# Query, key and value products of a two-block transformer: one step of the layernorm beside them is placed earlier

## The chip, the cores and the metric

The kernel runs on one core of one Trainium2 chip. TensorE, VectorE, ScalarE, GpSimd and SyncE each work through an instruction list of their own and meet through semaphores. In the profile they are PE (with PEld for its weight loads), DVE, ACT, POOL and SP. SP computes nothing: it issues nearly all DMAs. The metric is the device time of one execution in microseconds (us), lower is better; 2537.11 us is the median of three runs of the kernel before.

## The reference, cut to what matters

Eight batches of 512 rows of 512 float32 values go through a cross-attention block (L0) and then through a second block with self-attention, cross-attention and an MLP. The change is in the part between L0 and self-attention:

```python
def _ln(x):                                      # B, N, H = 8, 512, 512
    mu = jnp.mean(x, axis=-1, keepdims=True)
    var = jnp.var(x, axis=-1, keepdims=True)
    return (x - mu) * jax.lax.rsqrt(var + 1e-6)
x = _L0_xcond_ref(x, ...)                        # x1 in the kernel, kept in DRAM
x_norm = _ln(x) * (1 + scale_a[:, None]) + shift_a[:, None]
qkv = x_norm @ W_qkv + b_qkv                     # 512 x 1536 weights
q, k, v = jnp.split(qkv, 3, axis=-1)
```

## The kernel before, in words

The program is six stages: prepare, l0, qkv, attention, cross, mlp. Each stage has a `run` that says in which order its steps come, and every engine walks the same `run` with its own version of each step. So the order on all engines follows from where `run` places a step. Steps that need several places are generators, and `next(...)` emits their next piece. The last steps of a stage are woven with the first of the following one: `following` is the attention stage inside `Qkv.run`.

Float32 products are made of three matmuls of rounded parts (hi by hi, hi by lo, lo by hi), for each of four chunks of 128, so a product of 128 by 512 is 12 matmuls. For each batch `Qkv.run` has 12 products: m = 0 to 3 for the queries, 4 to 7 for the keys, then t = 0 to 3 for the values. They take turns in three PSUM banks. A q or k product is drained by ACT (line 1596, hi part, into `out_parts`) and then by DVE (line 1537, lo part), and SP stores both to DRAM (line 1518, 512 KB). ACT has two `out_parts` buffers in batch 0 and three later, so the drain of a product waits until the store of the product two or three before it has landed. DVE drains a value product (line 1549) and SP stores it (line 1523).

Beside the products of batch b, the layernorm of batch b+1 is made in `Norm`, 14 pieces handed out with `next(turning)`:

- piece 1: SP loads the batch's rows, 1 MB, into the one buffer `norm_x` (line 302), once PE has turned the batch before it out of that buffer and the rows of x1 are stored
- pieces 2 to 5: DVE takes statistics of four tiles (BN_STATS, line 312); the first waits for the load
- piece 6: DVE aggregates them (line 316), and POOL makes the reciprocal deviation (lines 337, 339)
- pieces 7 to 10: DVE normalises the four tiles in place (line 321)
- pieces 11 to 14: PE turns `norm_x` by transposes (line 354), ACT scales, shifts and rounds (lines 377, 379), DVE makes the lo part (line 329). These follow product m = 7 and the first three value products.

Which product a piece follows is in `STEPS_AT`, a table from m to a number of pieces. `weave(turning)` empties what is left at a batch's end. Self-attention begins to fetch its stacks of queries and keys (lines 1745 and 1748, six DMAs of 256 KB each, with a memset of DVE, line 1815) at the end of batches 3 and 4 and after m = 4 of batch 4: `next(following)`. Batch 0 also has the last rows of L0 beside it: PE projects the last four tiles between m = 5 and m = 6, and DVE adds them to the residual (line 1265).

Of the kernel before, what the change touches and what calls it, by code (L numbers as in the profile page):

```python
# [12 lines left out]
B, N, D = 8, 512, 512  # L13
# [92 lines left out]
def braid(*generators):  # L106

    left = [g for g in generators if g is not None]
    while left:
        for g in list(left):  # L110
            if next(g, StopIteration) is StopIteration:
                left.remove(g)
        if left:
            yield


def weave(*generators):
    for _ in braid(*generators):
        pass


def after(steps, generator):
    for _ in range(steps):
        yield
    yield from generator


def some(steps, generator):
    for _ in range(steps):
        next(generator, None)  # L130
        yield
# [293 lines left out]
class Prepare:  # L425
# [90 lines left out]
    def run(self, s, following):  # L516
        def splits(l, first, n):
            for i in range(first, first + n):
                s.split(self.piece_at[l] + i)
                yield  # L520

        def modulations(*sources):
            for i in sources:
                yield from s.modulation(i)

        s.begin()
        s.statistics()
        yield from braid(s.turn(0), after(1 + TT, s.parts(0)), after(2, splits(1, 0, G)), after(2, modulations(0)))
        yield from braid(s.keys(0), splits(1, G, G), s.turn(1), after(1, modulations(1)))
        yield from braid(s.values(0), modulations(2, 3), after(1, s.modulate()), some(10, following))  # L530
        yield from braid(s.parts(1), some(13, following), after(4, splits(0, 0, 2 * G)))
        yield from s.keys(1)
        yield from braid(some(1, following), s.values(1))
# [908 lines left out]
class Qkv:  # L1442


    STEPS_AT = {0: 1, 2: 2, 3: 2, 4: 1, 5: 2, 6: 2, 7: 1}

    def __init__(self, k, w, x_in, x_ready, mods_ready):
        self.k, self.w = k, w
# [24 lines left out]
    def run(self, s, following):  # L1473
        s.begin()

        def splits():
            for m in range(G):
                s.split(self.w_at + m)
                yield

        yield from braid(s.turn(0), after(Norm.HEAD, splits()))
        for b in range(B):
            turning = s.turn(b + 1) if b + 1 < B else iter(())
            for m in range(2 * G):
                if b == 0:
                    s.split(self.w_at + G + m)
                s.product(b, m)
                for _ in range(self.STEPS_AT.get(m, 0)):
                    next(turning, None)
                if b >= B - 3:  # L1490
                    weave(some(2 if b == B - 1 else 1, following))
                elif b == B - 4 and m == G:
                    next(following)
                yield
            for t in range(NT):
                s.value(b, t)
                next(turning, None)
                if b >= B - 3:
                    weave(some(2 if b == B - 1 else 1, following))
                yield  # L1500
            weave(turning)
            if B - 6 < b < B - 3:
                next(following)

# [910 lines left out]
```

## Time and profile before

| | |
|---|---|
| median of 3 runs | 2537.11 us (2529.11 to 2539.09) |
| the profiled execution's own time | 2532.49 us |
| its span (first to last instruction) | 2530.7 us |
| mean granted TensorE clock | 0.983 |
| the qkv stage in the trace | about 499 to 809 us |
| PE idle between 500 and 812 us, named waits | 8.7 us |

The busy share of an engine says how full it is. What bounds a stretch is read from who waits last there: a wait of PE counts when PE is otherwise full. Durations in the timeline are of single instructions; PE starts a 512-column matmul about every 0.23 us though each lasts about 0.39 us, since they are pipelined. In the chain, "issue" is time in which an engine waited for nothing that the trace shows.

### The profile page before, as it was taken

Reading aid. Unit: us, or ns where it says so; the run is one execution under the profiler, and the core shown is the slowest. Engines: PE = TensorE matmul, PEld = TensorE weight load, DVE = VectorE, ACT = ScalarE, POOL = GpSimd, SP = SyncE. Lnnn points to the kernel's source line nnn. Section 1 sums busy time; section 2 is a strip of 40 time slices with the busy share of each in tenths; the row PEclk is TensorE's granted clock in tenths of the full one; section 3 lists DMA queues with packets and bytes.
Section 4 is the critical chain, followed back from the end, with each engine's and each line's share of the span. In section 5 each row is a group of like instructions: output and inputs, shape, how many; then the busy total and the mean of one; then the engine's idle time right before and its main releaser. Section 6 shows DMA issues by size and latency. Waiting matters only on the chain.

```text
span 2530.7 us, 32358 instructions
## 1 busy us (share of the span) xinstructions
PE 2389.8 (94%) x12056; PEld 1675.6 (66%) x12056; DVE 1393.1 (55%) x2463; ACT 1025.3 (41%) x1831; POOL 580.2 (23%) x324
## 2 busy tenths in 40 slices
PE   6879999899999899999998899999999999999999
PEld 5656666578776344444444566666688888888887
DVE  4566666744565877777777566666642222232221
ACT  3454454423323555555554343444442332233232
POOL 2101111200000466666665311121111001101100
PEclk9899999999999899999999999999999999999999
DMA  6687787564664455656553497777431101110110
GB/s 211 192 214 221 213 222 217 165 209 176 208 206 149 106 133 129 157 134 157 131 139 89 125 237 184 204 212 202 155 88 59 59 1 59 59 58 1 59 42 17
DMA packets 261323, 354.19 MB, mean 140 GB/s; under 512 B 61027, under 2 KB 109243, under 8 KB 261166
## 3 DMA queue, kind: packets, MB, share of 16 engines
q1 hardware_dynamic: 259998, 348.27, 48.9%
q0 software_dynamic: 1168, 3.85, 0.4%
q8 instruction: 96, 1.57, 0.3%
q14 instruction: 61, 0.50, 0.1%
HBM read 233.78 MB, written 116.69 MB: 138 GB/s over the span
## 4 chain that ended last, share of the span: by engine, by line
PE 78%; DVE 7%; DMA 6%; ACT 3%; issue 3%; SPq 2%; POOL 0%; ACTq 0%; DVEq 0%; POOLq 0%
PE banks L396 40%; PE banks L2213 14%; PE banks L1913 6%; PE banks L1935 4%; PE banks L1892 4%; PE banks L1953 2%; DMA norm_x<-x 2%; PE banks L354 2%; PE banks L1322 2%; PE banks L1336 2%; PE banks L1343 2%; DVE negated_max L1827 1%; DVE negated_max L1221 1%; DVE norm_stats L312 1%; DMA norm_x<-in_x 1%
## 5 line engine op out<-in xcount | busy, mean ns | idle before, releaser
L1997 ACT ACTIVATE self_exponentials<-banks 128x512 f32<-128x512 f32 x512 | 286.3, 595 | 280.0 <-PE banks L1953 136.2
L1827 DVE TENSOR_REDUCE negated_max<-banks 128x1 f32<-128x512 f32 x512 | 330.7, 677 | 95.9 <-PE banks L1892 94.4
L2213 PE MATMUL banks<-mlp_w_down_hi,out_parts 128*128 128x512 f32 x1024 | 333.8, 389 | 0.1
L1793 POOL TENSOR_TENSOR self_exponentials<-self_exponentials,self_exponentials 128x2048 f32<-128x2048 f32 x63 | 289.7, 4599 | 187.9 <-ACT self_exponentials L1997 187.9
L337 POOL TENSOR_SCALAR norm_rstd<-norm_mean_var 128x4 f32<-128x4 f32 x32 | 8.0, 250 | 1341.6 <-DVE norm_mean_var L316 1341.6
L2170 DVE TENSOR_TENSOR out_parts<-wide,out_parts 128x512 fp32r<-128x512 f32 x128 | 92.0, 719 | 371.7 <-ACT out_parts L2242 371.7
L2232 ACT ACTIVATE wide<-banks,bias_columns 128x512 f32<-128x512 f32 x128 | 88.3, 690 | 426.0 <-PE banks L396 426.0
L1913 PE MATMUL banks<-self_query_stack,self_key_stack 98*128 98x512 f32 x512 | 232.9, 458 | 9.7 <-ACT self_exponentials L1997 6.8
L1913 PEld LDWEIGHTS banks<-self_query_stack,self_key_stack 98*128 98x128 f32 x512 | 97.2, 191 | 190.6 <-ACT self_exponentials L1997 155.8
L2213 PEld LDWEIGHTS banks<-mlp_w_down_hi,out_parts 128*128 128x128 f32 x1024 | 192.2, 188 | 40.5 <-DVE cross_last_x_rows L1265 0.5
L1892 PE MATMUL banks<-self_key_stack,self_query_stack 96*128 96x512 f32 x512 | 208.2, 410 | 9.0 <-DVE negated_max L1827 6.7
L2213 PE MATMUL banks<-mlp_w_down_lo,out_parts 128*128 128x512 f32 x512 | 199.2, 389 | 0.0
L1221 DVE TENSOR_REDUCE negated_max<-banks 128x4 f32<-128x308 f32 x256 | 121.1, 473 | 66.8 <-PE banks L396 65.9
L1935 PE MATMUL banks<-self_exponentials,self_values 128*32 128x512 f32 x1024 | 137.0, 607 | 0.5 <-ACT self_exponentials L1997 0.5
L312 DVE BATCH_NORM_STATS2 norm_stats<-norm_x 128x6 f32<-128x512 f32 x128 | 84.9, 674 | 75.6 <-DMA norm_x<-x 68.5
L377 ACT ACTIVATE wide<-banks,modulation_columns 128x512 f32<-128x512 f32 x96 | 74.6, 777 | 114.6 <-PE banks L354 109.1
L1892 PEld LDWEIGHTS banks<-self_key_stack,self_query_stack 96*128 96x128 f32 x512 | 98.8, 193 | 27.5 <-DVE negated_max L1827 10.5
L1404 ACT ACTIVATE cross_exponentials<-banks 77x512 f32<-77x512 f32 x128 | 75.6, 593 | 99.6 <-PE banks L1322 99.5
L1207 DVE SCALAR_TENSOR_TENSOR out_parts<-banks,bias_columns,out_parts 128x512 fp32r<-128x512 f32 x64 | 47.9, 748 | 118.1 <-ACT out_parts L1380 117.6
L1596 ACT ACTIVATE out_parts<-banks,bias_columns 128x512 fp32r<-128x512 f32 x64 | 44.1, 690 | 162.8 <-PE banks L396 136.0
L329 DVE TENSOR_TENSOR x_lo<-wide,x_hi 128x512 fp32r<-128x512 f32 x80 | 61.0, 763 | 88.1 <-ACT x_hi L379 88.0
L1404 ACT ACTIVATE L_exponentials<-banks 77x512 f32<-77x512 f32 x128 | 75.5, 592 | 83.9 <-PE banks L1322 83.9
(208 smaller groups left out, 5339.5 us busy)
## 6 DMA issues: line engine op xcount, KB each, us to landing
L_query_stack<-q_parts_L SPq DMA_DIRECT2D x96, 256.0 KB, 4.9
norm_x<-x SPq DMA_DIRECT2D x24, 1024.0 KB, 7.9
self_query_stack<-q_parts_self SPq DMA_DIRECT2D x96, 256.0 KB, 4.1
self_key_stack<-k_parts_self SPq DMA_DIRECT2D x96, 256.0 KB, 6.4
cross_query_stack<-q_parts_cross SPq DMA_DIRECT2D x96, 256.0 KB, 4.8
x_rows<-x SPq DMA_DIRECT2D x23, 1024.0 KB, 6.1
x<-x_rows SPq DMA_DIRECT2D x22, 1024.0 KB, 5.0
q_parts_L<-out_parts SPq DMA_DIRECT2D x32, 512.0 KB, 4.9
```

The source lines that it names most:

```text
L312: e.bn_stats(stats[:, t, :], xn[:, t, :]).then_inc(self.stats.sem, 1)
L396: mm = e.matmul(out_ap, l, r, start=i == 0, stop=i == len(terms) - 1)
L1221: e.tensor_reduce(k.nm[n % 2][:, t:GH * NT:NT], k.bank[:, bk, 0:GH * S].rearrange("p (h k) -> p h k", k=S), AX_X, ALU.max, negate=True).th ...
L1404: e.activation(self.p[:, i % self.HEADS_KEPT, :], k.bank[0:S, self.scores.of["score", i], :], ACT.Exp, scale=SCALE).then_inc(self.exp.sem, 1)
L1793: e.tensor_tensor(self.p[kt - 1][:], self.p[kt - 1][:], self.p[kt][:], ALU.add).then_inc(self.paired.sem, 1)
L1827: e.tensor_reduce(k.nm[n % 2][:, h * NT + t:h * NT + t + 1], k.bank[:, self.max_banks.of["max", i], :], AX_X, ALU.max, negate=True).then_i ...
L1892: e.matmul(k.bank[:, bk, :], self.q[n % 4][0:ST, h, t * P:(t + 1) * P], self.keys[n % 4][0:ST, h, :], start=True, stop=True).then_inc(self ...
L1913: e.matmul(k.bank[:, bk, :], self.keys[n % 4][0:ST_MAX, h, kt * P:(kt + 1) * P], self.q[n % 4][0:ST_MAX, h, :], start=True, stop=True).the ...
L1935: mm = e.matmul(k.bank[h * HD:(h + 1) * HD, bk, :], self.v[n % 3][:, kt, h * HD:(h + 1) * HD], self.p[kt][:, h, :], start=kt == 0, stop=kt ...
L1997: e.activation(self.p[kt][:, h, :], k.bank[:, self.scores.of["score", i], :], ACT.Exp, scale=SCALE).then_inc(self.exp.sem, 1)
L2170: e.tensor_tensor(h[:, 1, :], k.wides[k.wide_turns.of["up", i]][:], raw(h[:, 0, :]), ALU.subtract).then_inc(self.lo.sem, 1)
L2213: mm = e.matmul(bank, l, w, start=j == 0 and q == 0, stop=j == JC - 1 and q == 2)
```

## The change

`STEPS_AT` is changed, and the first piece of a batch's norm (the load) is taken at the end of the batch before instead of after product m = 0. For batch 1 it is taken before the loop.

```diff
-    STEPS_AT = {0: 1, 2: 2, 3: 2, 4: 1, 5: 2, 6: 2, 7: 1}
+    STEPS_AT = {1: 2, 2: 2, 3: 1, 4: 2, 5: 2, 7: 1}
...
+        def loading(b):
+            turning = s.turn(b) if b < B else iter(())
+            next(turning, None)
+            return turning
+
         yield from braid(s.turn(0), after(Norm.HEAD, splits()))
+        turning = loading(1)
         for b in range(B):
-            turning = s.turn(b + 1) if b + 1 < B else iter(())
             for m in range(2 * G):
...
             weave(turning)
+            turning = loading(b + 2)
             if B - 6 < b < B - 3:
                 next(following)
```

The lists of PE, ACT and POOL are the same, instruction for instruction; those of SP and DVE have the same instructions in another order. Lines after 1480 have numbers that are 6 higher in the changed kernel (1518 becomes 1524, 1537 becomes 1543).

SP at the start of batch 0: `x<-x_rows` is a batch of L0's output, `weight_stage` the pieces of the qkv weights, `q_parts_self` the stores of the first query products. Before:

```order
L1165 DMA x<-x_rows 128x4x512
L253 DMA weight_stage_52<-in_L_xcond_W_qkv 128x4x128
L1518 DMA q_parts_self<-out_parts_64 128x2x512
L302 DMA norm_x<-x 128x4x512
L253 DMA weight_stage_49<-in_L_xcond_W_qkv 128x4x128
L1518 DMA q_parts_self<-out_parts_65 128x2x512
```

and in the changed kernel:

```order
L1165 DMA x<-x_rows 128x4x512
L302 DMA norm_x<-x 128x4x512
L253 DMA weight_stage_52<-in_L_xcond_W_qkv 128x4x128
L1524 DMA q_parts_self<-out_parts_64 128x2x512
L253 DMA weight_stage_49<-in_L_xcond_W_qkv 128x4x128
L1524 DMA q_parts_self<-out_parts_65 128x2x512
```

The load of batch 1's rows has moved ahead of a weight piece and of the first query store.

SP from the last value store of batch 3 to the second query store of batch 4, where self-attention's first fetch lies. Before:

```order
L1523 DMA v_self<-qkv_value_rows_144 128x512
L1745 DMA self_query_stack_148<-q_parts_self 32x4x512 x3
L1748 DMA self_key_stack_152<-k_parts_self 32x4x512 x3
L1518 DMA q_parts_self<-out_parts_64 128x2x512
L302 DMA norm_x<-x 128x4x512
L1518 DMA q_parts_self<-out_parts_65 128x2x512
```

and in the changed kernel:

```order
L1529 DMA v_self<-qkv_value_rows_144 128x512
L302 DMA norm_x<-x 128x4x512
L1751 DMA self_query_stack_148<-q_parts_self 32x4x512 x3
L1754 DMA self_key_stack_152<-k_parts_self 32x4x512 x3
L1524 DMA q_parts_self<-out_parts_64 128x2x512
L1524 DMA q_parts_self<-out_parts_65 128x2x512
```

The load has moved ahead of the six fetches and of the first store. In the other batches it moves ahead of one query store only.

DVE from product m = 1 to m = 7 of batch 4; the memset belongs to self-attention's second fetch. Before:

```order
L1537 SCALAR_TENSOR_TENSOR out_parts_65<-banks,bias_columns,out_parts_65 128x512
L1537 SCALAR_TENSOR_TENSOR out_parts_66<-banks,bias_columns,out_parts_66 128x512
L312 BN_STATS norm_stats<-norm_x 128x6 x2
L1537 SCALAR_TENSOR_TENSOR out_parts_64<-banks,bias_columns,out_parts_64 128x512
L312 BN_STATS norm_stats<-norm_x 128x6 x2
L1537 SCALAR_TENSOR_TENSOR out_parts_65<-banks,bias_columns,out_parts_65 128x512
L316 BN_AGGR norm_mean_var<-norm_stats 128x2 x4
L1815 MEMSET self_key_stack_153 2x2048
L1537 SCALAR_TENSOR_TENSOR out_parts_66<-banks,bias_columns,out_parts_66 128x512
L321 TENSOR_SCALAR norm_x<-norm_x,norm_mean_var,norm_rstd 128x512 x2
L1537 SCALAR_TENSOR_TENSOR out_parts_64<-banks,bias_columns,out_parts_64 128x512
L321 TENSOR_SCALAR norm_x<-norm_x,norm_mean_var,norm_rstd 128x512 x2
```

and in the changed kernel:

```order
L1543 SCALAR_TENSOR_TENSOR out_parts_65<-banks,bias_columns,out_parts_65 128x512
L312 BN_STATS norm_stats<-norm_x 128x6 x2
L1543 SCALAR_TENSOR_TENSOR out_parts_66<-banks,bias_columns,out_parts_66 128x512
L312 BN_STATS norm_stats<-norm_x 128x6 x2
L1543 SCALAR_TENSOR_TENSOR out_parts_64<-banks,bias_columns,out_parts_64 128x512
L316 BN_AGGR norm_mean_var<-norm_stats 128x2 x4
L1543 SCALAR_TENSOR_TENSOR out_parts_65<-banks,bias_columns,out_parts_65 128x512
L321 TENSOR_SCALAR norm_x<-norm_x,norm_mean_var,norm_rstd 128x512 x2
L1821 MEMSET self_key_stack_153 2x2048
L1543 SCALAR_TENSOR_TENSOR out_parts_66<-banks,bias_columns,out_parts_66 128x512
L321 TENSOR_SCALAR norm_x<-norm_x,norm_mean_var,norm_rstd 128x512 x2
L1543 SCALAR_TENSOR_TENSOR out_parts_64<-banks,bias_columns,out_parts_64 128x512
```

Statistics, aggregation and normalisation each stand one drain (one product) earlier. The same shift is in every batch from 0 to 6; the transposes stay where they were.

## Rows read from the trace of the kernel before

**Rows 1.** The page, part 1: busy time, share of the span, instructions.

```profile
PE 2389.8 (94%) x12056; PEld 1675.6 (66%) x12056; DVE 1393.1 (55%) x2463; ACT 1025.3 (41%) x1831; POOL 580.2 (23%) x324
```

**Rows 2.** Stretches of the stage: us, busy PE, PEld, DVE, ACT, POOL, PEclk, DMA, GB/s.

```profile
575.00:610.00 35.00, 35.00 (x163) 28.85 (x162) 16.10 (x29) 11.42 (x17) 1.26 (x2) 1.00 0.50 181
645.00:680.00 35.00, 31.85 (x145) 25.72 (x145) 17.89 (x28) 9.61 (x14) 1.26 (x2) 1.00 0.71 213
715.00:750.00 35.00, 33.58 (x156) 27.47 (x155) 22.27 (x40) 9.77 (x15) 0.62 (x3) 1.00 0.49 177
```

**Rows 3.** Waits of PE, 500 to 812 us: total, times, longest.

```profile
PE banks L396 <- DVE L_last_x_rows L1265: 4.0, 2, 3.1
PE banks L354 <- DVE norm_x L321: 3.3, 2, 1.9
PE banks L396 <- DVE out_parts L1537: 1.4, 2, 1.2
```

**Rows 4.** Chain that ended last, batch 0: start us, us, what.

```profile
506.96 7.83 DMA q_parts_self<-out_parts
...
516.43 4.60 DMA q_parts_self<-out_parts
...
521.11 0.70 ACT out_parts L1596
...
522.50 0.99 DVE norm_x L321 x2
```

**Rows 5.** Timeline of SP, batch 0: start us, us, engine line, op, what.

```profile
498.40 0.46 SPq L253 DMA_DIRECT2D weight_stage<-in_L_xcond_W_qkv  x1
...
505.41 0.46 SPq L302 DMA_DIRECT2D norm_x<-x  x1
```

**Rows 6.** Timeline, end of batch 1 and start of batch 2; brackets hold idle time.

```profile
578.40 6.74 SPq L1523 DMA_DIRECT2D v_self<-qkv_value_rows  x3
...
588.79 0.47 SPq L302 DMA_DIRECT2D norm_x<-x  x1
...
595.85 1.29 DVE L312 BATCH_NORM_STATS2 norm_stats<-norm_x 128x6 f32<-128x512 f32 x2 [2.11 <-DMA norm_x<-x]
```

**Rows 7.** The line of the loads: time from issue to landing.

```profile
DMA to landing us min/median/max: 5.6/8.3/11.2
```

**Rows 8.** Timeline of SP, end of batch 3 and start of batch 4.

```profile
644.36 9.96 SPq L1523 DMA_DIRECT2D v_self<-qkv_value_rows  x4
...
657.55 0.38 SPq L1518 DMA_DIRECT2D q_parts_self<-out_parts  x1
```

**Rows 9.** Chain that ended last, batch 4: start us, us, what.

```profile
657.97 10.81 DMA norm_x<-x
...
673.36 1.01 DVE self_key_stack L1815
...
679.10 4.35 PE banks L396 x12
...
683.89 2.78 PE banks L396 x12
```

**Rows 10.** Timeline of ACT, batch 4: drains that waited for a store.

```profile
666.32 0.69 ACT L1596 ACTIVATE out_parts<-banks,bias_columns 128x512 fp32r<-128x512 f32 x1 [4.19 <-DMA q_parts_self<-out_parts]
670.17 0.69 ACT L1596 ACTIVATE out_parts<-banks,bias_columns 128x512 fp32r<-128x512 f32 x1 [3.16 <-DMA q_parts_self<-out_parts]
```

**Rows 11.** Timeline of PE, batch 4: where it resumes, with its idle time.

```profile
670.80 0.50 PE L396 MATMUL banks<-x_hi,w_qkv_hi 128*128 128x512 f32 x1 [1.24 <-DVE out_parts L1537]
...
678.44 0.66 PE L354 MATMUL banks<-identity,norm_x 128*128 128x128 f32 x4 [1.91 <-DVE norm_x L321]
```

**Rows 12.** Busy time and granted clock just after, columns as in rows 2.

```profile
680.00:684.00 4.00, 4.00 (x15) 3.08 (x14) 1.21 (x2) 0.69 (x2) 0.00 (x0) 0.59 1.04 286
```

**Rows 13.** Timeline of DVE, batch 5: its wait for the load.

```profile
708.66 1.29 DVE L312 BATCH_NORM_STATS2 norm_stats<-norm_x 128x6 f32<-128x512 f32 x2 [5.40 <-DMA norm_x<-x]
```

**Rows 14.** Chain that ended last, batch 5: POOL's reciprocal deviation.

```profile
714.33 1.05 POOL norm_rstd L339
```

## The prediction, made before the changed kernel ran

> **What bounds the kernel now.** I read the page first: PE is busy 94% of the span [rows 1], so a stretch gets shorter only where PE waits or runs slowly. The change touches only SP's and DVE's order inside the qkv stage, so next came the busy time by stretches of it. Batches 1 to 3 leave nothing: in the stretch from 575 to 610 PE is busy 35.00 of 35 us [rows 2]. The stretches of batch 4 (31.85 of 35) and batch 5 (33.58) have holes. Third, the waits of PE in the stage: 4.0 us on DVE's last additions of L0 (two, the longest 3.1), 3.3 us on DVE's normalisation, in front of a transpose (two, the longest 1.9, so the other 1.4), and 1.4 us on DVE's drains (two, the longest 1.2) [rows 3]. That is 8.7 us in all. Fourth, the chain of waits says what lies behind them, and twice it is a load of `norm_x` or what queues beside it.
>
> In batch 0 the chain goes through stores of query products, because ACT may not drain product m = 3 before the store of m = 1 has landed (two buffers). That store took 7.83 us, that of m = 3 took 4.60 [rows 4]. The 1 MB load was issued 1.55 us ahead of the slow one (505.41 against 506.96) [rows 5]. The chain ends in ACT's drain of m = 5 at 521.11 and two normalisations at 522.50, and only behind them can DVE make the additions that PE's projection waits 3.1 us for.
>
> In batch 4 the load goes out behind six fetches of self-attention and a store, and needs 10.81 us [rows 9]. DVE, which works in order, sits before the statistics until 668.8 while the drain of m = 3 stands behind them. PE resumes m = 6 after 1.24 us and, since everything is late, the transposes after 1.91 us more [rows 11]. Just behind that a product of 12 matmuls takes 4.35 us where the next takes 2.78 [rows 9], with a granted clock of 0.59 in that stretch, a mix of 2.4 GHz and 1.2 GHz [rows 12]. Batch 5 repeats it more mildly: DVE waits 5.40 us for its load [rows 13].
>
> **The change part by part.** Nothing is added or removed. One load and eight groups of DVE instructions per batch move, and their durations (two statistics 1.29 us [rows 6], two normalisations 0.99 us [rows 4]) are paid as before, beside PE.
>
> *Batches 1 to 3.* The load leaves right behind the last value store, at 585.1 (578.40 + 6.74) instead of 588.79, 3.7 us sooner. It took 7.06 us to the statistics (588.79 to 595.85) [rows 6]; by that it lands at 592.2. The statistics stand one product (2.8 us) earlier: DVE gets to them at 593.74 - 2.8 = 590.9 and waits about 1.2 us where it waited 2.11. PE has no hole there to give back: 0.
>
> *Batch 0.* The load now stands on SP before the weight piece of 498.40 [rows 5], 7 us sooner. With the longest landing of any load, 11.2 us [rows 7], it is in by 509.6, with 7.06 by 505.5. The store of m = 1 no longer runs behind it. I price it at 4.60 us, like the store of m = 3, which had no load near it: it lands at 511.6 instead of 514.8. ACT's drain (0.70), DVE's (about 0.7: 522.50 less 521.11 less 0.70) and the store of m = 3 (again 4.60, with 0.1 between) follow, so m = 5 is drained from 517.8 instead of 521.11, 3.3 us sooner. PE waits 3.1 us for the addition behind it, so all of the wait goes. Two normalisations still stand between that drain and the additions (the other pair now, 0.99 us as before). The ends: 0, if the weight pieces and not the load held the store up, and 3.1. I take 3.1, since the load is four times a weight piece. The other 0.9 us of those 4.0 stays: there PE waits for the tile that it has just finished. What is late next is PE itself.
>
> *Batch 4.* The load leaves at 654.3 (644.36 + 9.96) [rows 8] and not at 657.97. It lands between 659.9 and 665.5 (5.6 to 11.2 us [rows 7]); with 7.06 us at 661.4, against 668.8. The price is paid by the store of m = 0, issued at 657.55 [rows 8], on which ACT's drain of m = 3 waited until 666.32 [rows 10]: it now has 1 MB more ahead of it. It lands between 666.3 and 668.8, when all of that load and store was in before; I take 668.8. Then 0.69 + 0.75 us of drains free the bank at 670.25, and PE goes on at 670.3 instead of 670.80. Aggregation ends at 670.5. POOL's two instructions end about 1.6 us later (the longer is 1.05 [rows 14]), two normalisations about 673.1, the memset starts at 673.6 (before, 673.36 [rows 9]). Behind it come 1.8 us for the memset and its pause, 0.75 for a drain and 0.99 for two normalisations, and no longer a second drain with a second pair: the transposes start at 677.1 instead of 678.44. Gain 1.3 us. With the store at 666.3 it is 1.8, because the drain of m = 4 then waits for the next store, at 670.17 as before [rows 10]. The third term is the slow product: 4.35 - 2.78 = 1.57 us. It follows two pauses of PE of 1.24 and 1.91; now 0.7 and about 1.1 remain. I take it as given back, bounds 0 and 1.6.
>
> On the queue the Trainium skill (DMA: Bandwidth & Descriptors, section Queues, rings and completion order) says that on each DMA engine descriptors are consumed in ring order. The trace agrees as far as it goes: in batch 4 the store issued before the load landed first, at 666.3 against 668.8. The rule speaks against the change there, since the megabyte put in front delays the six fetches and every query store.
>
> On the clock the skill (TensorE: Matmul & The Clock Gate, Part 1: The HAM clock gate) says that the gate follows how busy the array was of late. By that the fall belongs to the pauses in front of it; the trace shows 0.59 behind them and cannot say which pause did it. With the rule the term is 1.6, without it 0.
>
> *Batch 5.* Seven fetches and a store, each at least 0.4 us on SP, no longer stand ahead of the load, so it lands at least 3.4 us sooner; the wait of 5.40 us [rows 13] shrinks below 2, and normalisation ends one product (2.8 us) earlier than now. There is no memset between. PE's 1.4 in front of the transposes and 0.2 at the drain go: 1.6 us, bounds 0 and 1.6. Batch 6 has no hole.
>
> **Sum.** 3.1 + 1.3 + 1.6 + 1.6 = 7.6 us off the profiled execution's 2532.49 (span 2530.7 and 1.8 around it): 2524.9. That execution is 4.6 us below the median of the runs, which spread from 2529.11 to 2539.09. The middle of the four executions shown is 2534.8, and less 7.6 that is 2527.2, which I forecast. The bounds of the terms add up to 0 and 8.1.
>
> **The rivals.**
> A, only batch 0 gains. The queue has the same 4 MB to move in batch 4 whatever the order, and the query stores arrive late instead of the load: the wait of DVE becomes one of ACT. For it: ACT already waits 4.19 and 3.16 us for stores there [rows 10]. Against it: those waits ended at 666.3, 2.5 us before the load. Then batches 4 and 5 give nothing, and it is -3.1: 2531.7.
> B, slower. The statistics now stand ahead of the drain of m = 2. PE wants that bank for m = 5, two products (5.6 us) after m = 2 ends. In batch 2 that drain was over at 593.74, behind 1.44 us of drains, so its product ended near 592.3, so PE wants it at 597.9, and the load must be in by 597.9 - 0.75 - 1.29 = 595.9, 10.8 us after its issue at 585.1. From there it decides: a load of 11.2 us costs PE 0.4, and in seven batches 2.8, and if each pause also costs a slow product of 1.6 us, 14. Against it: 7.06 us here. Time without the gains: 2534.8 + 2.8 = 2537.6, with the slow products 2549.
> C, nothing: the holes are filled from elsewhere (batch 0 by the weight pieces, the rest as in A): 2534.8.
> D, more than the named waits: with the stage earlier, pauses or slow products after 812 us fall out differently. The trace has no row for it; as much again as the forecast's 7.6 gives 2519.6.
>
> **How the numbers follow.** Forecast 0.56, A 0.20, B 0.08 (half of it with slow products), C 0.08, D 0.08. About 0.5% (12.7 us) is what a measurement of this kernel can tell from no change. The forecast's 7.6 us is inside, but medians of runs spread over 10 us can stray by 5: I give 0.05 of its share to faster, with D's 0.07 that makes 0.12. Slower is B's hard half with a little of C's scatter, 0.05. The rest, 0.83, is within. The range goes from 2517 (D, or the forecast with 10 us of scatter) to 2538 (B without slow products).
>
> **What would show it.** In the trace of the changed kernel: the load of batch 1 issued near 498 and the store of m = 1 at 4 to 5 us; the 3.1 us wait on L0's last additions gone; in batch 4 the load landing before 666, the drain of m = 3 waiting for a store until about 668.8 (less 3 us for what batch 0 gave), PE's wait before the transposes about 1.1, no stretch with a clock below 0.9; in batch 5 no wait before the transposes. PE's named waits in the stage fall from 8.7 us to about 3. It is wrong if the waits stay with new names, if batches 1 to 3 show PE below 35.00 of 35, or if the stage is 7 us shorter and the whole is not.

## The result and the profile after

The changed kernel took 2525.83 us (median of 15 runs, 2519.86 to 2530.95) beside 2534.59 us for the kernel before (15 runs): ratio 0.9966, 95% interval 0.9954 to 0.9979, 8.8 us less where 7.6 were forecast. A second comparison, below, gave 0.9977 (0.9964 to 0.9989), 6.1 us. The kernel before compared with itself gave 0.9986 (0.9972 to 1.0). So a comparison of this kind can be off by some 3 us, and what each mechanism is worth is read from the traces.

Waits of PE in the changed kernel, 500 to 812 us (total, times, longest), to set beside [rows 3]:

```profile
PE banks L396 <- DVE out_parts L1543: 3.3, 2, 1.9
PE banks L354 <- DVE norm_x L321: 1.0, 1, 1.0
PE banks L396 <- DVE L_last_x_rows L1265: 0.9, 1, 0.9
```

The 4.0 us on L0's last additions have become 0.9 and the 3.3 before the transposes 1.0, but the waits on drains grew from 1.4 to 3.3. In sum 8.7 became 5.2, not 3. (In this stretch there is also a pause of 0.5 us at 809.86 in self-attention's own products, which begin sooner now.)

Batch 0, timeline of SP and then of ACT in the changed kernel (start us, us, engine, line, what; idle time in brackets), to set beside [rows 4, 5]:

```profile
499.12 0.37 SPq L1165 DMA_DIRECT2D x<-x_rows  x1
499.54 0.50 SPq L302 DMA_DIRECT2D norm_x<-x  x1
...
507.51 0.60 SPq L1524 DMA_DIRECT2D q_parts_self<-out_parts  x1
```

```profile
512.34 0.69 ACT L1602 ACTIVATE out_parts<-banks,bias_columns 128x512 fp32r<-128x512 f32 x1 [1.24 <-DMA q_parts_self<-out_parts]
...
517.64 0.69 ACT L1602 ACTIVATE out_parts<-banks,bias_columns 128x512 fp32r<-128x512 f32 x1 [1.84 <-DMA q_parts_self<-out_parts]
```

The store of m = 1 now takes 4.8 us (507.51 to 512.34) instead of 7.83, and m = 5 is drained at 517.64. The chain that ended last has no DMA in it any more here:

```profile
500.22 27.48 PE banks L396 x120
527.70 0.02 issue
527.72 0.70 DVE L_last_x_rows L1265
```

Batch 4, timelines of SP, DVE, ACT and PE in the changed kernel, to set beside [rows 8 to 11]:

```profile
652.06 0.43 SPq L302 DMA_DIRECT2D norm_x<-x  x1
652.61 2.20 SPq L1751 DMA_DIRECT2D self_query_stack<-q_parts_self  x3
654.85 1.75 SPq L1754 DMA_DIRECT2D self_key_stack<-k_parts_self  x3
656.69 12.82 SPq L1524 DMA_DIRECT2D q_parts_self<-out_parts  x4
```

```profile
654.42 0.75 DVE L1543 SCALAR_TENSOR_TENSOR out_parts<-banks,bias_columns,out_parts 128x512 fp32r<-128x512 f32 x1 [0.51 <-ACT out_parts L1602]
...
659.49 1.29 DVE L312 BATCH_NORM_STATS2 norm_stats<-norm_x 128x6 f32<-128x512 f32 x2 [1.59 <-DMA norm_x<-x]
```

```profile
667.61 0.69 ACT L1602 ACTIVATE out_parts<-banks,bias_columns 128x512 fp32r<-128x512 f32 x1 [7.77 <-DMA q_parts_self<-out_parts]
```

```profile
669.13 0.50 PE L396 MATMUL banks<-x_hi,w_qkv_hi 128*128 128x512 f32 x1 [1.87 <-DVE out_parts L1543]
...
675.91 0.65 PE L354 MATMUL banks<-identity,norm_x 128*128 128x128 f32 x4 [1.05 <-DVE norm_x L321]
...
708.25 0.50 PE L396 MATMUL banks<-x_hi,w_qkv_hi 128*128 128x512 f32 x1 [1.46 <-DVE out_parts L1543]
```

The kernel before had, on DVE and on SP:

```profile
668.81 1.28 DVE L312 BATCH_NORM_STATS2 norm_stats<-norm_x 128x6 f32<-128x512 f32 x2 [5.90 <-DMA norm_x<-x]
```

```profile
654.43 1.35 SPq L1745 DMA_DIRECT2D self_query_stack<-q_parts_self  x3
655.81 1.38 SPq L1748 DMA_DIRECT2D self_key_stack<-k_parts_self  x3
```

The load lands 7.4 us after its issue and DVE waits 1.6 us for it instead of 5.9. But the query store issued at 656.69 lands 10.9 us later (667.6), where it was 8.8 before (657.55 to 666.3), and ACT waits 7.77 us for it. It was also issued late: DVE's part of the drain was done at 655.17 (654.42 + 0.75), but SP was issuing the six fetches until 656.60. Behind the load they took 4.0 us of SP's time (652.61 to 656.60) where they had taken 2.8 (654.43 to 657.19). PE's pause at m = 6 grew from 1.24 to 1.87; the one before the transposes shrank from 1.91 to 1.05. The last row is batch 5, where the same pause grew from 0.2 to 1.46 and the one before the transposes, 1.4, is gone. The slow product is absent: the granted clock of the stretch in [rows 12] is now 1.00:

```profile
680.00:684.00 4.00, 4.00 (x22) 3.25 (x21) 1.45 (x3) 2.16 (x4) 0.00 (x0) 1.00 1.04 392
```

The lengths of the pieces, each worked out from two drains of ACT in the trace (the drain of m = 0 of a batch to that of the next; the stage is from there in batch 0 to the drain of m = 7 in batch 7; the last column is from there to the span's end):

| profiled execution | batch 0 | batches 1 to 3 | batch 4 | batch 5 | stage | behind it |
|---|---|---|---|---|---|---|
| before | 48.85 | 103.79 | 39.85 | 39.76 | 292.52 | 1734.8 |
| before, again | 50.76 | 103.80 | 37.75 | 39.65 | 292.24 | 1732.5 |
| changed | 45.32 | 103.84 | 38.04 | 39.17 | 286.64 | 1731.5 |
| changed, again | 45.27 | 103.84 | 37.46 | 38.67 | 285.51 | 1732.6 |
| load_only | 45.49 | 103.80 | 38.52 | 41.26 | 289.34 | 1735.5 |
| steps_only | 49.25 | 105.16 | 41.58 | 44.07 | 300.33 | 1731.1 |
| batch0_only | 45.33 | 103.80 | 37.94 | 39.87 | 287.21 | 1734.6 |
| rest_only | 50.24 | 103.84 | 37.30 | 38.68 | 290.33 | 1735.6 |
| spread | 45.33 | 103.83 | 34.62 | 37.44 | 281.49 | 1734.2 |
| before_spread | 49.12 | 103.80 | 34.60 | 37.44 | 285.23 | 1731.5 |

Of the 8.0 us between the first two spans of before and changed (2530.7 and 2522.7), the stage gives 5.9 and what lies behind it 3.3, while batch 0 began 1.2 later.

### The profile page after: what moved, and what is told of

The parts are those of the page before. It is cut to its first block, busy times and chain, and to the rows that moved or that the text cites. A ratio compares the mean times of both kernels' runs of the same rounds, so it can differ in the third digit from the quotient of the medians.

```text
span 2522.7 us, 32358 instructions
## 1 busy us (share of the span) xinstructions
PE 2386.7 (95%) x12056; PEld 1675.2 (66%) x12056; DVE 1395.4 (55%) x2463; ACT 1024.2 (41%) x1831; POOL 580.5 (23%) x324
## 4 chain that ended last, share of the span: by engine, by line
PE 81%; DVE 6%; DMA 4%; ACT 4%; issue 3%; SPq 2%; POOL 0%; ACTq 0%; DVEq 0%; POOLq 0%
PE banks L396 42%; PE banks L2219 14%; PE banks L1919 6%; PE banks L1941 4%; PE banks L1898 4%; PE banks L1959 2%; PE banks L354 2%; PE banks L1322 2%; PE banks L1336 2%; PE banks L1343 2%; DMA norm_x<-x 2%; DMA q_parts_self<-out_parts 1%; DVE negated_max L1221 1%; DVE negated_max L1833 1%; DVE norm_x L321 1%
## 5 line engine op out<-in xcount | busy, mean ns | idle before, releaser
L2219 PEld LDWEIGHTS banks<-mlp_w_down_lo,out_parts 128*128 128x128 f32 x512 | 96.1, 188 | 19.9
```

The lines of the kernel that those rows point to most:

```text
L2219: mm = e.matmul(bank, l, w, start=j == 0 and q == 0, stop=j == JC - 1 and q == 2)
```

## The experiments

### Parts of the change

**load_only**: the early load, the DVE pieces where they were.

```diff
-    STEPS_AT = {1: 2, 2: 2, 3: 1, 4: 2, 5: 2, 7: 1}
+    STEPS_AT = {2: 2, 3: 2, 4: 1, 5: 2, 6: 2, 7: 1}
```

> The early loads of the change with DVE's statistics and normalisation where they were before. Theory (batch 0's store chain gives 3.4 us, the shift of the DVE pieces is what batches 4 and 5 need): batch 0 as in the changed kernel, the 3.1 us wait of PE on the last additions gone; in batch 4 the load lands near 659.5, but the second pair of normalisations stands behind the drain of m = 6 again, so PE waits 1.9 to 2.5 us before the transposes and the slow product stays. Total -3 to -5 us against before, 3 to 6 us above the changed kernel. Rival (the place of the load is all): the same as the changed kernel, -8 to -9 us.

Measured: 2531.23 us against 2533.78, ratio 0.9987 (0.9974 to 1.0). Batch 0 is 45.49 long: the load alone gives all of the gain there but 0.2 us. In batch 4 PE waits 1.54 at m = 6 and 1.89 before the transposes, and in batch 5 1.84 and 1.4, so batch 5 is even 1.5 us longer than before. In total it is 2.6 us less, where 3 to 5 were expected. The pauses before the transposes are the expected ones: here an early load without early statistics only makes the stores late. The slow product that I expected to stay in batch 4 was absent, though the two pauses sum to 3.43 us, more than the 3.15 of the first trace of before.

**steps_only**: the DVE pieces early, the load after m = 0 as before.

```diff
-    STEPS_AT = {0: 1, 2: 2, 3: 2, 4: 1, 5: 2, 6: 2, 7: 1}
+    STEPS_AT = {0: 1, 1: 2, 2: 2, 3: 1, 4: 2, 5: 2, 7: 1}
```

> The DVE pieces one product earlier, the load after m = 0 as before. Theory: DVE reaches the statistics before the load has landed in every batch, with the drain of m = 2 behind them. In batch 4 the load lands near 668.8, the drain of m = 2 ends near 671, and PE, which wants its bank at 666.7 for m = 5, waits about 4 us; the same in batch 5, about 2 us in batch 0; in batches 1 to 3 the load lands in time (7 us) and PE waits under 0.3 us. Total +4 to +12 us against before. Rival (the shift of the DVE pieces is what gives the gain, the load hardly matters): -3 us or better.

Measured: 2539.53 us against 2533.78, ratio 1.0017 (1.0005 to 1.0029), 5.8 us more; the stage is 7.8 us longer. DVE in batch 4, with the drain of m = 2 behind the statistics:

```profile
671.15 1.28 DVE L312 BATCH_NORM_STATS2 norm_stats<-norm_x 128x6 f32<-128x512 f32 x2 [8.52 <-DMA norm_x<-x]
672.36 0.73 DVE L1537 SCALAR_TENSOR_TENSOR out_parts<-banks,bias_columns,out_parts 128x512 fp32r<-128x512 f32 x1
```

and PE in batch 4, held at m = 5:

```profile
673.14 0.79 PE L396 MATMUL banks<-x_hi,w_qkv_hi 128*128 128x512 f32 x1 [3.86 <-DVE out_parts L1537]
```

In batch 5 the longest pause is not at m = 5 but at a product of self-attention woven in there, whose maximum (`negated_max`) DVE also had to take behind the statistics:

```profile
716.41 0.59 PE L1892 MATMUL banks<-self_key_stack,self_query_stack 96*128 96x512 f32 x1 [4.54 <-DVE negated_max L1827]
```

Behind both pauses stands a stretch at a granted clock near a half (columns as in [rows 12]):

```profile
672.00:676.00 4.00, 2.85 (x7) 2.28 (x8) 3.86 (x10) 0.69 (x1) 0.61 (x2) 0.54 0.36 141
...
716.00:720.00 4.00, 3.52 (x8) 2.54 (x9) 4.00 (x11) 0.52 (x1) 0.17 (x1) 0.58 0.34 131
```

This is my rival B made real. Its mechanism works as described, and the changed kernel escapes it because the load moved with the statistics. Batches 1 to 3 lose 1.4 us in all, more than the under 0.3 each that I allowed.

**batch0_only**: the change in batch 0 alone (`LATE_AT` is the table of before).

```diff
         turning = loading(1)
         for b in range(B):
+            if b:
+                turning = s.turn(b + 1) if b + 1 < B else iter(())
...
-                for _ in range(self.STEPS_AT.get(m, 0)):
+                for _ in range((self.LATE_AT if b else self.STEPS_AT).get(m, 0)):
...
-            turning = loading(b + 2)
```

> The change in batch 0 alone (load of batch 1's rows before the loop, DVE pieces of batch 0 early), the rest as before. Theory: PE's wait of 3.1 us on the last additions of L0 goes and nothing else in the stage changes: -3.4 us at the end of batch 0 and at the end of the stage, total -3 to -4 us. Rival (the gain behind the stage, 3 us in the changed kernel's trace, follows any shortening of the stage): total -6 or better.

Measured: 2529.32 us against 2533.78, ratio 0.9984 (0.997 to 0.9999), 4.5 us less where 3 to 4 were expected. Batch 0 is 3.52 us shorter. Behind the stage nothing is gained (1734.6 against 1734.8), so the rival gets no support from this trace: here the shorter stage did not shorten what follows. A surprise is batch 4: its order is that of before and its pauses are 0.95 and 1.91, yet it is 1.9 us shorter, because the slow product did not occur (1.6 us) and the first pause was 0.3 shorter.

**rest_only**: the change in batches 1 to 7 alone.

```diff
-        turning = loading(1)
+        turning = s.turn(1)
...
-                for _ in range(self.STEPS_AT.get(m, 0)):
+                for _ in range((self.STEPS_AT if b else self.LATE_AT).get(m, 0)):
```

> The change in batches 1 to 7 alone, batch 0 as before. Theory: batch 4 gives 1.8 us (1.6 of it the slow product behind the transposes), batch 5 gives 0.5: -2.3 us at the end of the stage, total -2 to -3 us. Rival (slow product not due to the pauses): -0.7 us at the end of the stage and a granted clock below 0.7 somewhere in batch 4.

Measured: 2534.73 us against 2533.78, ratio 1.0006 (0.9993 to 1.0019), 1.0 us more: the -2 to -3 us expected were not there. The stage of its trace is 2.2 us shorter, which is the expected number, but made of other terms. In its trace the batches after batch 0 are 3.6 us shorter than in the first trace of before (2.55 and 1.08 in batches 4 and 5), but batch 0, with the order of before, is 1.4 longer, since the half clock fell there, behind PE's pause:

```profile
529.00:533.00 4.00, 3.12 (x8) 2.53 (x9) 1.42 (x3) 0.00 (x0) 0.00 (x0) 0.57 0.34 131
```

(Columns as in [rows 12].) The half clock in batch 4 that the rival asked for did not occur. And batch 0 began 5.7 us later than in the first trace of before, in work that the edit does not touch.

### The same kernels again

**after_again** is the changed kernel, without an edit.

> The changed kernel once more. If the whole is the sum of its parts as measured alone (batch 0 alone -4.5, the rest alone +1.0): -3 to -6 us, near the 5.9 us that the stage got shorter in the first trace. If the parts help one another: again -8 to -10 us. In the stage the same landmarks as in its first trace within 0.3 us, the slow product in batch 4 absent; behind the stage the clock may fall elsewhere, by up to 3 us either way.

Measured: 2526.87 us against 2532.98, ratio 0.9977 (0.9964 to 0.9989), 6.1 us less. That lies between the two cases that I had set against each other, at the edge of the first: the parts alone add up to -3.5 us (-4.5 and +1.0), and the 2.6 us more are no more than the kernel before differs from itself. So it stays open whether the parts help one another. The stage is 285.51 long against 286.64: the pauses at m = 6 were shorter (2.3 us in sum instead of 3.3), which is more than the 0.3 us I allowed. Before the transposes PE waits 1.04 again.

**before_again** is the kernel before, without an edit.

> The kernel before once more, against itself. Ratio 1.000 with its interval: what a comparison of five rounds can tell. In the trace: if the slow product behind the transposes of batch 4 belongs to the two pauses of PE (1.24 and 1.91 us), it is there again with a granted clock near 0.6; if it is a matter of chance, the pauses are there and it may be absent. The stage has the same length as in the first trace within 0.3 us but for that product (1.6 us).

Measured: 2530.33 us against 2532.98, ratio 0.9986 (0.9972 to 1.0), where 1 was expected: 2.7 us that no edit made. The trace tells most. The pauses of PE in batch 4 are there (0.76 and 1.91):

```profile
672.34 0.50 PE L396 MATMUL banks<-x_hi,w_qkv_hi 128*128 128x512 f32 x1 [0.76 <-DVE out_parts L1537]
...
679.98 0.66 PE L354 MATMUL banks<-identity,norm_x 128*128 128x128 f32 x4 [1.91 <-DVE norm_x L321]
```

and the slow product is not; the granted clock was 1.00 there and 0.57 behind the pause of batch 0 instead:

```profile
524.00:528.00 4.00, 3.52 (x8) 2.83 (x9) 1.02 (x2) 0.00 (x0) 0.00 (x0) 0.57 0.30 120
...
680.00:684.00 4.00, 4.00 (x22) 3.42 (x23) 1.87 (x3) 1.55 (x3) 0.00 (x0) 1.00 1.04 233
```

### Where the fetches lie

**spread**: the changed kernel, with self-attention's first three fetches behind m = 7 of batches 2, 3 and 4.

```diff
-                elif b == B - 4 and m == G:
+                elif B - 7 < b < B - 3 and m == 2 * G - 1:
                     next(following)
...
             turning = loading(b + 2)
-            if B - 6 < b < B - 3:
-                next(following)
```

> The changed kernel with self-attention's three fetches moved from the end of batch 3, the middle and the end of batch 4 to behind product m = 7 of batches 2, 3 and 4. Theory (the fetches, not the load, hold up the query stores of batches 4 and 5): the store of m = 0 lands 3 to 6 us after its issue, the drains of m = 3 wait less than 1 us, PE's waits of 1.9, 1.0 and 1.5 us in batches 4 and 5 are gone and the stage is 4.4 us shorter than in the changed kernel; total -10 to -13 us against before. Rival (the crowd only moves): the load for the next batch now goes out behind a fetch and the value stores, lands 3 to 5 us later, and PE waits at the drains of m = 2 or before the transposes instead; total within 2 us of the changed kernel.

Measured: 2518.87 us against 2532.98, ratio 0.9942 (0.9928 to 0.9957), 14.1 us less and the fastest of all. That is a little more than the 10 to 13 expected. It lies 8.0 us under the changed kernel of the same comparison, and the two intervals do not meet. The stage accounts for 5.2 us of it against the first trace of the changed kernel and 4.0 against the second (4.4 were forecast); where the rest comes from is not shown. Busy time by stretches, columns as in [rows 2]:

```profile
645.00:680.00 35.00, 35.00 (x163) 28.87 (x162) 17.80 (x29) 11.01 (x16) 1.27 (x2) 1.00 0.71 227
680.00:715.00 35.00, 35.00 (x163) 28.91 (x162) 20.69 (x36) 10.38 (x15) 1.27 (x2) 1.00 0.61 205
```

PE has no hole left in batches 4 and 5, which are 3.42 and 1.73 us shorter than in the changed kernel. The query stores land sooner. The median of the eight issued between 640 and 720 us, from issue to landing, is 3.0 us here, 10.0 in the changed kernel and 8.1 in the kernel before. Their line in `spread` (KB of one, median us to landing):

```profile
q_parts_self<-out_parts SPq DMA_DIRECT2D x8, 512.0 KB, 3.0
```

The drain of m = 3 of batch 4 waits for its product and for no store:

```profile
659.70 0.69 ACT L1600 ACTIVATE out_parts<-banks,bias_columns 128x512 fp32r<-128x512 f32 x1 [2.03 <-PE banks L396]
```

**before_spread**: the kernel before with the same places of the fetches.

> The kernel before with the same new places of the fetches, its norm untouched. Theory: batches 4 and 5 lose their pauses (1.24, 1.91, 0.2, 1.4 us and the slow product), batch 0 keeps its 3.1 us: -4 to -6.5 us at the end of the stage. Then the change's own gain in batches 4 and 5 is one that the place of the fetches gives too, and only its gain in batch 0 is its own. Rival (the late load in batch 4 is late by itself): the pauses stay above 2 us in sum.

Measured: 2525.41 us against 2532.98, ratio 0.9971 (0.9957 to 0.9984), 7.6 us less. The stage is 7.3 us shorter than in the first trace of before, beyond the 4 to 6.5 expected. Batches 4 and 5 are 34.60 and 37.44 long, the same as in `spread` to 0.02 us, and batch 0 keeps its pause of 3.3 us. So the stalls of batches 4 and 5 come from where the fetches lie, whatever the norm's order. The edit moves more than the transfers: DVE's memset (1.76 us) and SP's time for issuing the fetches move with them. The store times above show that the transfers are a large part of it; how much the other two add, no run separates. With the fetches away, the change is worth batch 0's gain: the two stages differ by 3.74 us (285.23 less 281.49), 3.79 of it in batch 0.

## Why the prediction was right, and where it was not

The time, the sign and the size hold: 8.8 and 6.1 us measured, 7.6 forecast. The mechanism holds in batch 0. For batches 4 and 5 one of my signs of being wrong came up in part: the waits stayed with new names (on drains 3.3 us instead of 1.4). Term by term:

- *Batch 0, 3.1 us: right, by the mechanism given.* Batch 0 is 3.5 us shorter in each of the four traces with the early load and early statistics there (45.27 to 45.33), and `load_only` (45.49) shows that the place of the load does it. I priced the store of m = 1 at 4.60 and its trace says 4.8; m = 5 was to be drained 3.3 us sooner, and came 4.7 us sooner, since the store of m = 1 was also issued 0.6 us sooner and that of m = 3 took 3.7 us (513.90 to 517.6) instead of 4.60, counted from the start of the batch (517.64 less 504.54 against 521.11 less 503.36).
- *Batches 1 to 3, nothing: right* (103.84 against 103.79).
- *Batch 4, the pauses, 1.3 us (bounds 1.3 and 1.8): too large.* I let the store of m = 0 land at 668.8 at the latest, by the kernel before's times. Set back by the 2.3 us that the batch now begins sooner, that is 666.5; it landed at 667.6. The step that failed is that the store would still be issued at 657.55, which is 655.25 after the same shift: it was issued at 656.69, 1.4 us later, because the fetches behind the load kept SP longer. Why they did is not shown. So PE's pause at m = 6, which was to shrink to 0.7, grew to 1.87. The pause before the transposes came as said, 1.05. The two together are 2.92 against 3.15, a gain of 0.2. My sum gave 0 as the lower bound of all terms together, though this one had no lower bound under 1.3 in the working. Against `before, again`, which has no slow product, batch 4 of the changed kernel is 0.3 us longer in one trace and 0.3 shorter in the other: this step gave nothing that two traces can tell.
- *The slow product, 1.6 us: the step that failed in its reason.* It was taken as given back because it followed the two pauses. With pauses of the old size (the second 1.89 to 1.91) it occurred in one of four traces (before; not `before, again`, `load_only`, `batch0_only`, and `load_only` had the longest pauses of the four in sum). It is gone in both traces of the changed kernel, but the first trace of before was merely one that had it.
- *Batch 5, 1.6 us: half of it.* 0.6 and 1.1 us in the two traces against 39.76. The wait before the transposes went, as said, and the query store that is late here too gave back 1.46 and 0.95 at m = 6.
- *Behind the stage, nothing in the sum.* The first two traces differ by 3.3 us there. Over ten traces that stretch spans 1731.1 to 1735.6 us with no relation to the edit that I can see, and the kernel before alone differs by 2.3 from itself. So scatter is enough to explain it, and it happened to fall on the changed kernel's side; why the clock falls where it does was not settled.

So a part of the hit is luck. What the traces carry is 3.5 us in batch 0 and 0.2 and 1.3 in batches 4 and 5 together (77.21 and 76.13 against the 77.40 of `before, again`), where the forecast had 4.5; the rest of the measured 6.1 to 8.8 may lie in the slow products that the lost pauses no longer risk and in the error of a comparison, which the runs cannot separate.

Rival A (only batch 0 gains, the query stores arrive late instead) described batches 4 and 5 better than the forecast did: its mechanism is what the 7.77 us wait of ACT shows. On the Trainium skill's rule that descriptors are consumed in ring order (DMA: Bandwidth & Descriptors, Queues, rings and completion order), the trace now agrees with a size: with 1 MB more in front, the store's time from issue to landing rose from 8.8 to 10.9 us. Rival B did not occur in the changed kernel and did in `steps_only`.

The Trainium skill's rule on the clock (TensorE: Matmul & The Clock Gate, Part 1: The HAM clock gate), by which the gate follows how busy the array was, agrees in so far as the stretches near half clock in the qkv stage stood only behind pauses of PE, of 1.91 us (before), 3.16 to 3.35 (`rest_only`, `before, again`) and 3.86 and 4.54 (`steps_only`). It does not make a pause cost one each time: behind the pause of 3.1 to 3.4 us in batch 0, two of four traces had a slow stretch (`before, again` and `rest_only`, batch 0 at 50.76 and 50.24; before and `before_spread`, 48.85 and 49.12, had none).

## What to carry to other kernels

A load that is moved forward in a full queue changes place with others: in batch 4 what was issued behind it landed later, and as those were stores that free buffers, the wait moved from the reader of the load (5.9 us to 1.6) to the writer's drain (4.19 to 7.77). Count the issuing engine's time as well as the bytes. So ask what crowds the queue: in batches 4 and 5 moving the bulk transfers that have no near deadline (here the fetches) removed all pauses, where moving the urgent load removed few. In the whole kernel the two changes alone gave about the same (7.6 and 6.1 us in one comparison, with intervals that overlap), since only the load's place helps batch 0, and together they gave 14.1. A term that rests on one slow stretch seen in one trace should be given as a chance and not as a microsecond figure, and the same kernel should be compared with itself before differences of 3 us are explained.

## What the runs showed that I had not expected

- The 1.6 us of a product at half clock comes and goes between executions of one kernel, at the same pause of 1.91 us before the transposes. Batch 4 took 39.85 and 37.75 us (the other 0.5 us is the pause at m = 6).
- Moving three groups of six fetches of 256 KB from where the next batch's load and query stores go out to the value products, where only 256 KB stores go out, removed every pause of PE in batches 4 and 5 (5.3 us against the first trace of before in batch 4, 1.6 of it the slow product, and 2.3 in batch 5).
- The kernel before against itself came out at 0.9986 with an interval that ends at 1.0: the interval alone does not cover all the scatter between two such comparisons.
